# Cross attention on one core: the output projection split into three single-pass products, and scores and weighted sums taken in turn by halves

## The reference

```
qh, kh, vh = heads(x @ Wq), heads(ctx @ Wk), heads(ctx @ Wv)   # 8 heads, 2048 tokens, 128 wide each
sim  = qh kh^T / sqrt(128);  sim = (sim - mean) * 1.5 + mean
attn = softmax(sim);  out = attn vh          # per head 2048 x 2048, then 2048 x 128
y    = concat_heads(out) @ Wout + bout       # Wout: 1024 x 256
```

## Time and profile before

| | |
|---|---|
| median of 3 runs | 1330.17 us (1330.01 to 1332.84) |
| profiled execution | 1332.3 us |
| its span, first to last instruction | 1330.2 us, mean granted TensorE clock 0.990 |
| busy: PE, PEld, DVE, ACT, POOL | 97%, 81%, 77%, 67%, 68% of the span |
| cross attention's slots | from about 392 us to about 1206 us |

### The profile page before, as it was taken

How to read it: one execution, slowest core, us unless ns; L and a number is a source line. 1 busy time by engine, 2 the same in 40 slices (tenths; PEclk the granted TensorE clock), 3 DMA queues, 4 the chain that set the end, 5 groups by cost and what they waited for, 6 DMA issues and landing times. The chain is left out here.

```text
span 1330.2 us, 22729 instructions
## 1 busy us (share of the span) xinstructions
PE 1287.7 (97%) x8358; PEld 1077.1 (81%) x8358; DVE 1023.5 (77%) x1628; ACT 895.9 (67%) x1315; POOL 907.9 (68%) x645
## 2 busy tenths in 40 slices
PE   5999999999999999999999999999999999988998
PEld 4688888888887788888888888888888888777998
DVE  6355498759317889999999999999999899985554
ACT  4555433425655878878778778778787777775774
POOL 2544410225410899989989999999999989863553
PEclk9999999999999999999999999999999999997999
DMA  6703032246764989988888888888888888796672
GB/s 219 104 6 74 4 101 81 67 130 245 208 233 140 247 213 231 221 196 216 215 203 215 216 201 218 215 196 221 214 201 217 201 191 208 185 252 244 203 230 76
DMA packets 172377, 241.35 MB, mean 181 GB/s; under 512 B 34179, under 2 KB 78085, under 8 KB 172272
## 3 DMA queue, kind: packets, MB, share of 16 engines
q1 hardware_dynamic: 155040, 208.11, 62.0%
q10 hardware_dynamic: 15184, 25.96, 5.7%
q0 software_dynamic: 2048, 5.90, 1.1%
HBM read 64.79 MB, written 41.32 MB: 80 GB/s over the span
## 5 line engine op out<-in xcount | busy, mean ns | idle before, releaser
L1217 POOL TENSOR_TENSOR xa_pT<-xa_moved,xa_pT 128x1024 fp32r<-128x1024 f32 x246 | 589.0, 2428 | 27.1 <-ACT xa_pT L1735 26.0
L1557 PE MATMUL xa_S<-xa_kT,xa_qT 128*128 128x512 f32 x1536 | 389.1, 401 | 1.2 <-ACT xa_probs L1741 1.2
L1741 ACT ACTIVATE xa_probs<-xa_S,xa_mx_nb_rinv 128x1024 f32<-128x1024 f32 x256 | 285.9, 1117 | 146.8 <-DVE xa_mx_nb_rinv L1339 146.8
L1574 PE MATMUL xa_O<-xa_pT,xa_v 128*128 128x512 f32 x1536 | 377.2, 394 | 2.9 <-DVE xa_pT L1392 2.6
L1336 DVE TENSOR_REDUCE xa_mx_nb_rinv<-xa_S 128x1 f32<-128x1024 f32 x256 | 305.3, 1211 | 78.1 <-PE xa_S L1557 78.0
L1574 PEld LDWEIGHTS xa_O<-xa_pT,xa_v 128*128 128x128 f32 x1536 | 289.0, 189 | 69.9 <-DVE xa_pT L1392 2.9
L1557 PEld LDWEIGHTS xa_S<-xa_kT,xa_qT 128*128 128x128 f32 x1536 | 288.5, 188 | 67.9 <-ACT xa_probs L1741 2.9
L1349 DVE STREAM_TRANSPOSE xa_tq<-xa_probs 128x1024 f32<-128x1024 f32 x256 | 316.7, 1238 | 15.0 <-ACT xa_probs L1741 7.3
L1735 ACT ACTIVATE xa_pT<-xa_moved 128x1024 fp32r<-128x1024 f32 x254 | 253.9, 1050 | 2.1 <-PE xa_O L1574 1.1
L506 PE MATMUL fw_pp<-fw_hT,fw_wqk 128*128 128x512 f32 x384 | 95.0, 405 | 4.3 <-DVE fw_hT L647 4.3
L506 PEld LDWEIGHTS fw_pp<-fw_hT,fw_wqk 128*128 128x128 f32 x384 | 73.4, 194 | 20.7 <-DVE fw_hT L647 3.0
(11 more groups left out here) (247 smaller groups left out, 1679.1 us busy)
## 6 DMA issues: line engine op xcount, KB each, us to landing
xa_moved<-xa_tq SPq DMA_DIRECT2D x508, 256.0 KB, 4.5
heads_k<-ci_outs SPq DMA_DIRECT2D x32, 256.0 KB, 2.0
heads_v<-ci_outs SPq DMA_DIRECT2D x32, 256.0 KB, 2.3
heads_q<-ci_outs SPq DMA_DIRECT2D x32, 256.0 KB, 2.4
xa_chunk<-heads_v ACTq DMA_DIRECT2D x32, 256.0 KB, 4.2
ex_w1s<-in_L_ffn_w_dram SPq DMA_DIRECT2D x8, 1024.0 KB, 7.3
ex_w2s<-in_L_ffn_w_dram SPq DMA_DIRECT2D x8, 1024.0 KB, 9.7
xa_chunk<-heads_q ACTq DMA_DIRECT2D x31, 256.0 KB, 4.2
```

Source lines behind the costliest of these rows:

```text
L1217: pool.tensor_tensor(quadrants(pT[LO], r), unit_moved(r), quadrants(pT[HI], r).bitcast(F32), ALU.subtract).then_inc(lo_ready, 1)
L1557: last = pe.matmul(banks[:, k % 2], qT[a][:, i // GT % 2, q], kT[b][h % 2][:, k * 512:(k + 1) * 512], start=(n == 0), stop=(n == 2))
L1574: last = pe.matmul(O[:], v[a][:, j * P:(j + 1) * P], pT[b][:, r % PRING, k], start=(j == 0 and n == 0), stop=(j == JT - 1 and n == 2))
L1741: act.activation(probs[:, unit % RING], S[:, score_banks(unit)].rearrange("p a b -> p (a b)"), ACT.Exp, bias=nb[:, s % 2:s % 2 + 1], scale ...
```

## The change

Three things are done together.

1. For groups 0 to 27 (heads 0 to 6, `SPLIT_GROUPS`) the output projection takes float32r operands in three products. ACT copies bank `xa_O` into a high tile, DVE subtracts that tile from the bank into a low tile (`output_low`, new), and `Wout`'s 128 rows of a head become a chunk ("w", h) of their own that ACT and POOL split. The weighted sums of the next group wait for `out_lo`, the end of DVE's subtraction, since it reads the bank. The last four groups stay as they were.
2. The two score halves and the two weighted halves of a slot are issued in turn (score, weighted, score, weighted), except in phase 0, where both scores come first.
3. Chunks are loaded straight into the place of their low part instead of a ring; the load for slot s + 1's chunk is issued by ACT at the end of slot s. The order of chunks is new. The ring's memory holds the split output tiles. `copy_oT` moves from the start of the phase 0 slot to the end of the phase 3 slot, behind its exponentials and ahead of its chunk.

```diff
+        SPLIT_GROUPS = SLOTS // GT - 4
+        def group_of_outputs(s):
+            g, phase = divmod(s - LAG - GT, GT)
+            return g if phase == 0 and 0 <= g < SPLIT_GROUPS else None
...
-            plan = {0: ("k", h + 1, 0), 1: ("q", h, 1), 2: ("k", h + 1, 1), 3: ("k", h + 1, 2), 4: ("v", h, 0),
-                    5: ("q", h, 2), 6: ("v", h, 1), 7: ("v", h, 2), 8: ("v", h, 3), 9: ("k", h + 1, 3),
-                    10: ("q", h, 3), 13: ("q", h + 1, 0)}
+            plan = {0: ("k", h + 1, 0), 1: ("q", h, 1), 3: ("k", h + 1, 1), 4: ("q", h, 2), 5: ("v", h, 0), 6: ("v", h, 1),
+                    7: ("v", h, 2), 8: ("v", h, 3), 10: ("q", h, 3), 11: ("w", h, 0), 12: ("k", h + 1, 2),
+                    13: ("q", h + 1, 0), 14: ("k", h + 1, 3)}
...
@@ VectorE
+            def output_low(g):
+                dve.wait_ge(oT_ready, g + 1)
+                if g:
+                    dve.wait_ge(y_mm, 2 * g)
+                dve.tensor_tensor(by_tile(oTs[LO][:]), by_quadrant(O[:]), by_tile(oTs[HI][:]).bitcast(F32),
+                                  ALU.subtract).then_inc(out_lo, 1)
...
             for s in range(END):
+                g = group_of_outputs(s)
+                if g is not None:
+                    output_low(g)
                 if s < SLOTS:
                     maxima(s)
@@ TensorE
+            def weighted(p, half):
+                g, q = divmod(p, GT)
...
+                if half == 0 and q == 0 and 0 < g <= SPLIT_GROUPS:
+                    pe.wait_ge(out_lo, g)
+                elif half == 0 and q == 0 and g:
+                    pe.wait_ge(oT_ready, g)
...
             def out_project(g, k):
-                if k == 0:
+                if k == 0 and g < SPLIT_GROUPS:
+                    pe.wait_ge(chunk_lo, place["w", g // 4, 0] + 1)
+                    pe.wait_ge(out_lo, g + 1)
+                elif k == 0:
...
+                    if g < SPLIT_GROUPS:
+                        for n, (a, b) in enumerate(PARTS):
+                            last = pe.matmul(output_bank(g, k)[:, m], oTs[a][:, t], wohs[b][:], start=(n == 0), stop=(n == 2))
...
                 if s < SLOTS:
-                    scores(s)
+                    scores(s, 0)
+                    if 0 <= p and p % GT:
+                        weighted(p, 0)
+                    scores(s, 1)
...
                 if 0 <= p < SLOTS:
-                    weighted(p)
+                    if s >= SLOTS or p % GT == 0:
+                        weighted(p, 0)
+                    weighted(p, 1)
@@ ScalarE
             for s in range(END):
                 p = s - LAG
-                if GT <= p <= SLOTS and p % GT == 0:
+                if GT <= p <= SLOTS and p % GT == 0 and group_of_outputs(s) is None:
                     copy_oT(p // GT - 1)
...
+                if group_of_outputs(s + 1) is not None:
+                    copy_oT(group_of_outputs(s + 1))
                 if s < SLOTS:
                     for c in chunks_of(s):
                         chunk_high(c)
+                    for c in chunks_of(s + 1) if s + 1 < SLOTS else ():
+                        if c[0] != "w":
+                            load(place[c])
```

More of the change, by code:

```diff
@@ L904, in cross_block @@
         first_in = [sem(f"xa_first_in{i}") for i in range(FIRST)]
-        chunk_in = [sem(f"xa_chunk_in{i}") for i in range(CRING)]
+        chunk_in = sem("xa_chunk_in")
         chunk_hi, chunk_lo = sem("xa_chunk_hi"), sem("xa_chunk_lo")
@@ L1063, in staged @@
                 return moved[:].rearrange("p r q j n -> p (r q j n)")[:, n * UNIT:(n + 1) * UNIT]
-            return chunk[:, n % CRING]
+            kind, h, part = order[n]
+            cols = slice(part * UNIT, (part + 1) * UNIT)
+            if kind == "k":
+                return raw_k[h % 2][:, cols]
+            if kind == "w":
+                return woh[:]
+            return raw_v[:, cols] if kind == "v" else raw_q[:, part % 2]
         def target(c, a):
@@ L1147, in _ @@
                 h, i = divmod(p, TILES)
-                if h and i == 7:
-                    sp.wait_ge(y_mm, 8 * h)
+                if h and i == 0:
+                    sp.wait_ge(chunk_lo, place["w", h - 1, 0] + 1)
                     sp.dma_start(woh[:], w_out[h * XD:(h + 1) * XD, :]).then_inc(wo_in, 16)
@@ L1542, in _, with scores @@
                 project_q(n)
-            def scores(s):
+            def scores(s, u):
                 h, i = divmod(s, TILES)
-                if i == 0:
+                if i == 0 and u == 0:
                     pe.wait_ge(chunk_lo, place[("k", h, 3)] + 1)
-                if i % GT == 0:
+                if i % GT == 0 and u == 0:
                     pe.wait_ge(chunk_lo, place[("q", h, i // GT)] + 1)
                 q = slice(i % GT * P, (i % GT + 1) * P)
[L1550 to L1554, removed]
-                    for n, (a, b) in enumerate(PARTS):
[L1556 to L1576, removed]
+                unit = 2 * s + u
@@ new lines, in scores @@
+                banks = S[:, score_banks(unit)]
+                if unit >= 2:
+                    pe.wait_ge(exp_done, unit - 1 if unit < PAIRED + 2 else unit - 2)
+                for n, (a, b) in enumerate(PARTS):
+                    for k in (2 * u, 2 * u + 1):
+                        last = pe.matmul(banks[:, k % 2], qT[a][:, i // GT % 2, q], kT[b][h % 2][:, k * 512:(k + 1) * 512],
+                                         start=(n == 0), stop=(n == 2))
+                last.then_inc(sim_done, 1)
@@ new lines, in weighted @@
+            def weighted(p, half):
+                g, q = divmod(p, GT)
+                if p == 0 and half == 0:
+                    pe.wait_ge(pj_out, UNITS)
+                if half == 0 and q == 0 and 0 < g <= SPLIT_GROUPS:
+                    pe.wait_ge(out_lo, g)
+                elif half == 0 and q == 0 and g:
+                    pe.wait_ge(oT_ready, g)
+                if half == 0 and g % 4 == 0:
+                    pe.wait_ge(chunk_lo, place[("v", g // 4, q)] + 1)
+                r = 2 * p + half
+                low_until(pe, r)
+                for k in range(2):
+                    j = 2 * (r % 8) + k
+                    for n, (a, b) in enumerate(PARTS):
+                        last = pe.matmul(O[:], v[a][:, j * P:(j + 1) * P], pT[b][:, r % PRING, k],
+                                         start=(j == 0 and n == 0), stop=(j == JT - 1 and n == 2))
+                last.then_inc(pv_done, 1)
@@ L1588, in out_project @@
                 for m in range(2):
-                    t = 2 * k + m
-                    last = pe.matmul(output_bank(g, k)[:, m], oT[:, t * P:(t + 1) * P], woh[:], start=True, stop=True)
+                    t = slice((2 * k + m) * P, (2 * k + m + 1) * P)
+                    if g < SPLIT_GROUPS:
+                        for n, (a, b) in enumerate(PARTS):
+                            last = pe.matmul(output_bank(g, k)[:, m], oTs[a][:, t], wohs[b][:], start=(n == 0), stop=(n == 2))
+                    else:
+                        last = pe.matmul(output_bank(g, k)[:, m], oT[:, t], woh[:], start=True, stop=True)
                 last.then_inc(y_mm, 1)
@@ L1701, in load @@
             def load(n):
-                if n - CRING >= FIRST:
-                    act.wait_ge(chunk_lo, n - CRING + 1)
-                for u in units_of(order[n]):
+                c = kind, h, part = order[n]
+                if kind == "k" and h >= 2:
+                    act.wait_ge(sim_done, 2 * TILES * (h - 1))
+                if kind == "q" and 4 * h + part >= 2:
+                    act.wait_ge(sim_done, 2 * GT * (4 * h + part - 1))
+                if kind == "v" and h == 0:
+                    for u in range(UNITS - OUTS, UNITS):
+                        if u % OUTS == part + 1 or part == QUADS - 1 and u % OUTS == 0:
+                            written(act, u)
+                if kind == "v" and h:
+                    act.wait_ge(pv_done, 2 * (TILES * h - GT + part) + 2)
+                for u in units_of(c):
                     written(act, u)
-                act.dma_start(chunk[:, n % CRING], source(order[n])).then_inc(chunk_in[n % CRING], 16)
+                act.dma_start(staged(n), source(c)).then_inc(chunk_in, 16)
             def chunk_high(c):
@@ L1712, in chunk_high @@
                     act.wait_ge(first_in[n], 16)
-                else:
[L1714 to L1724, removed]
+                elif kind == "w":
+                    act.wait_ge(wo_in, 16 * (h + 1))
+                    if h:
+                        act.wait_ge(y_mm, 8 * h)
+                else:
+                    act.wait_ge(chunk_in, 16 * (loaded.index(n) + 1))
                 act.activation(target(c, HI), staged(n), ACT.Copy).then_inc(chunk_hi, 1)
-                if FIRST + CRING <= n + 1 < len(order):
-                    load(n + 1)
             def high_part(r):
```

45 lines of the change are left out of this document (27 added, 18 removed).

## The result

The changed kernel takes 1402.44 us (median of 4, 1399.8 to 1407.04), the kernel before 1330.09 (median of 4). The ratio is 1.0544, 95% interval 1.0509 to 1.0578: 5.4% slower. The prediction was 1398, range 1374 to 1414. The profiled execution is the slowest of the four, 1407.04 us with a span of 1405.3, so 75.1 us over the span before, where the medians are 72.4 apart; its mean granted clock is 0.980, that of the other three 0.983 to 0.986.

What follows compares the result with a forecast made beforehand. PE was taken to bound the kernel: -8.8 + 50.9 + 20 + 6 = +68 us made 1400 against the profiled 1332.3, so 1398 against the median 1330.17. Its own range was 1385 to 1412, widened to 1374 to 1414.

Steps and rivals of the forecast that it cites:

- The bound: Attention: PE, busy 682.1 of 683.0 us, sets the pace; less PE work shortens the time, any PE wait adds.
- The projection, -8.8: Output projection: each of 56 half groups takes 0.713 us instead of 0.87, saving 8.8 us; bounds 0 to 10.
- The wait for the subtraction, +50.9: Phase 0: PE waits 1.85 us for DVE to free xa_O, 28 times, the first 0.91; bounds 48 to 65.
- The order of halves: Before phase 0's bank use: turns leave PE 4.16 us of work instead of 5.56, where DVE's chain would cost 0.45.
- Wout's chunk, +20: Heads 1 to 6: PE waits 3.4 us each for POOL's low part of Wout; bounds 18 to 24.
- The clock, +6: Behind the six 3.4 us waits for Wout: lower granted clock costs 1 us each; bounds 0 to 16.
- that rival (1438): The clock also falls behind the waits of about 1.5 us, losing 1.5 us for each of 27: 1438; chance 0.07.
- my two examples: Idle PE of 3.04 and 2.13 us, after narrow matmuls, was followed by a granted clock of 0.50.
- issuing the loads a slot ahead at nothing: Chunk loads issued a slot ahead have over 5 us, and no listed wait names them: cost nothing.

Runs made afterwards that it cites:

- e7: Changed kernel with old order of halves everywhere, query and Wout chunks a slot earlier, VectorE's phase 3 second transpose and subtraction before addition: 1325.57 us.
- e3: Kernel before with only the halves taken in turn (part 2), float32 projection and no subtraction: 1359.62 us, ratio 1.0213.
- e5: Changed kernel with part 2 undone, both scores then both weighted halves in every slot: 1357.49 us, ratio 1.0188.
- e6: Changed kernel with part 2 undone in all slots and the query and Wout chunks a slot earlier: 1331.95 us, ratio 0.9997.
- e1: Changed kernel with the query chunk in slot 16h + 9 and Wout's chunk in 16h + 10, one slot earlier: 1373.09 us, ratio 1.0309.
- e2: Changed kernel with the old order of halves in phase 3 slots alone: 1377.63 us, ratio 1.0348.
- e8: Changed kernel, turns kept, chunks a slot earlier, ScalarE's bank copy between its exponentials, VectorE's subtraction right behind its first transpose: 1349.56 us, ratio 1.013.
- e4: Changed kernel, chunks a slot earlier, old order in phase 3 alone, VectorE's second transpose and subtraction before addition there: 1338.46 us, ratio 1.006.

## Why the prediction was right

- **The bound.** PE paced the attention, and each new wait went on top of it: a group's 25.27 us are 23.59 of PE's own work and 1.68 of waiting (for the exponential and for the bank), and nothing of that came back.
- **The projection, -8.8.** Right. e7's group shows 23.60 against a worked 23.59. The row of true float32 (0.87 for two matmuls) was the right one to keep to: by the four-pass rule of the Trainium skill (FP8 and Floating Point Precision, TensorE Precision Notes) a group would have saved 0.48 instead of the 0.34 seen.
- **The wait for the subtraction, +50.9.** The mechanism was right to some hundredths of a us, its size 10% high. Net of the projection I had 1.85 - 0.31 = 1.54 a group, measured 1.33; over 27 intervals that is 5.7 us too much. I counted on starts of weight loads. In steady work such a load runs 0.23 us ahead of its matmul (724.35 and 724.58 in the timeline after); behind a wait both start together (730.33 for loads and matmuls), so the lead is made up again: 12 loads behind the wait at 570.55 span 2.60 us where 12 in steady work span 2.70. PE's matmuls wait 1.12 us there, its loads 1.55, and neither is the price: the group's length says 1.68 with the exponential's wait in it.
- **The order of halves as the cause of most of it.** e3, e5 and e6 settle it: turns alone cost 29.6 us on the kernel before; undoing them in the changed kernel gives about 45 us back.
- **Wout's chunk, +20.** 3.32 a head, worked out as 3.4. e1 takes it away with the clock's share.
- **The clock, +6.** 7.4 in this execution, behind five of six waits. The page TensorE: Matmul & The Clock Gate of the Trainium skill (Why this matters for your kernels) warns of idle gaps; here a gap of 1.12 us never cost the clock, so that rival (1438) is out, and one of 3.1 did in part. How often differs from run to run: the same six waits stand in e2, where the clock fell behind all six (groups of 29.2 to 30.6 us), and in e5, where it fell behind two (28.8 and 28.7 us, the other four 27.2). The price I took, 1 us each, was a guess between 0 and 2.6; a fall in dense work cost 1.5. Each fall more or less moves an execution by 1.5 us, which fits the spread of 7 us over the four executions and their clocks (0.980 to 0.986), though only one of the four has a trace. That my two examples followed narrow matmuls was no protection for dense work: in e3 a gap of 1.87 us behind dense matmuls cost the clock.
- **Left out, and why the total came out so near.** The table has 11.8 us ahead of the first subtraction and behind the last, of which my sum held 0.6. I costed issuing the loads a slot ahead at nothing, and didn't cost the last groups. The 5.7 too much for the wait hid half of that, so the 4 us between 1398 and 1402 are partly luck. Behind the last subtraction the four groups still take turns, with the copy back at the start of phase 0, and PE waits for it and for the last exponential; the clock falls there too:

```profile
1203.63 3.00 PE L1612 MATMUL xa_O<-xa_pT,xa_v 128*128 128x512 f32 x12 [0.49 <-ACT xa_oT L1801]
...
1234.81 1.94 PE L1646 MATMUL xa_S<-ident,ex_z 128*128 128x128 f32 x8 [2.86 <-ACT xa_probs L1792]
```

A hole of 2.07 us stood at that place before as well. e1, whose program differs there only in the place of one query chunk, needs 2.1 us more than before behind its last subtraction, so about 4.4 of the 6.6 belong to this execution: 2.8 of them lie in the two groups in which the clock falls behind the 2.86 us. The same hole in e1 (2.85 us) cost no clock.

At the start ScalarE, which now must see the last projections stored before it may issue a value load, waits for that once, and holds up its weights and exponential behind it:

```profile
ACT xa_pT L1786 <- DMA heads_q<-ci_outs: 2.8, 1, 2.8
```

Such a line (1.5 to 3.0 us) stands in every run with part 3 of the change and in neither the kernel before nor e3. From the first score to the first weighted sum of phase 0 the attention takes 71.4 us before, 72.8 with turns alone (e3), 72.6 to 73.2 with the old order and part 3 (e5 to e7), and 74.8 to 75.7 with turns and part 3 (the changed kernel, e1, e8). No run took this wait away, so how much of the start it makes stays open. 1.0 of the 5.2 us at the start had come before the first score, in work that the change doesn't touch.
- **Where expectations failed.** In e2 and e4 I took VectorE to be on time, as in the earlier trace rows, though the edit itself brought the next scores 1.4 us nearer. In e8 I left GpSimd out. Both are the same omission: I walked the repaired wait, not the phase behind it.

## What to carry to other kernels

When engines run in order, a single accumulator that is handed over (filled, copied out, filled again) makes a chain from the last dependent input to its release; compare that chain with the work that the bounding engine has left at that point, and do it again after every reordering, since issuing work earlier takes it out of the cover. Put the copies that free the accumulator ahead of work that nobody waits for, and prepare a rarely needed operand at least a slot before its first use: here these two edits and the old order turned a kernel 5.4% slower into one 0.5% faster, and the old order did most of it. A repair changes who is on time in the next phase, so walk a full period, not one wait.

## What the runs showed of the hardware

A hole of 3.1 us in otherwise dense matmuls (3.07 to 3.09 in all 18 cases) halved TensorE's granted clock behind five of six in the changed kernel's traced execution, six of six in e2's and two of six in e5's, for about 3 us and at a cost of about 1.5 us each (once in e2 for twice as long, 2.9 us). Holes of 1.12 us never did, 27 times in the changed kernel and 27 in e1; one of 1.87 us in e3 did. A weight load that was held back by a wait starts together with its matmul's record instead of 0.23 us ahead, so the waits of PEld overstate what a wait costs by a few tenths (0.5 for 0.28 in e6), and those of PE can understate it.
